# A normalisation of softmax rows moved for every fourth item from GpSimd to VectorE

## The chip, the cores and the metric

The kernel runs on one core of one Trainium2 chip. A core has TensorE (PE, matrix products), VectorE (DVE), ScalarE (ACT), GpSimd (POOL) and SyncE (SP, which here only issues DMAs). Each runs its own list of instructions in order, and they meet at semaphores. The metric is the time on the device in microseconds (us): the median of three runs is 1448.82, from 1447.1 to 1449.51.

## The reference

Four layers with a layer norm before each: graph attention over 16384 random edges and the loops, a mixture of 8 experts (top 2), a graph network, and a transformer block (attention with 8 heads, then 8 experts, top 1). The change lies in the attention of the last one. N is 1024 rows, D is 512, and a head has 64 columns:

```python
q = (x @ Wq + bq).reshape(B, S, NH, dh)      # k and v alike
scores = jnp.einsum('bqhd,bkhd->bhqk', q, k) / jnp.sqrt(jnp.float32(dh))
attn = jax.nn.softmax(scores, axis=-1)
ctx = jnp.einsum('bhqk,bkhd->bqhd', attn, v).reshape(B, S, D)
sa = ctx @ Wo + bo
x = _layernorm(x + sa, g1, beta1)            # then the experts, and a second layer norm
```

## The kernel before

Everything is computed in pairs of a high and a low half of fp32 numbers (H and L in the names), and a product is made of three products of halves. Stages follow each other; the one that matters is the second attention, from 876 to about 1172 us.

It works through 64 items. An item i is 128 queries of one head against all 1024 keys. Sixteen items (m = 0 to 15 in the code) belong to a pair of heads, hp = 0 to 3; four items with the same head and consecutive blocks make a group. Each engine has the order of its work written out by hand, in loops over hp and m that run ahead of each other by two or three items. The steps of an item:

- PE, head_scores (L1432): four matrix products into two of the banks 0 to 3 of PSUM. Done for item i + 3 while i is the current one.
- DVE, maximum (L1112): the negative row maximum, 128x1024 read from PSUM.
- ACT, head_exp (L731): the exponential into AP_[:, i % 4, :], with the row sums in denom. AP_ has four buffers.
- DVE, denominator (L1117): rden = 1 / denom, for item i + 2.
- POOL, normalise (L544): AP_ times rden, in place, 128x1024, for item i + 2.
- PE, head_transposes (L1443): eight transposes of 128x128 into banks 4 and 5. They wait for the normalisation of item i, and for the low halves of item i - 1, which empty those banks.
- ACT, head_hi (L576), and DVE, head_lo (L789): two instructions each, which copy the transposed block from PSUM to APH and the remainder to APL.
- PE, head_values (L1457, L1458, L1460): after four items, the products with V into bank 6, half of them in m % 4 == 3 and half in the next m % 4 == 0. ACT (L748) and DVE (L792, L1131) then split the result.

In between, in bank 7, PE makes what the next pair of heads needs (K in m = 1 and 3, Q in 5 and 13, V in 7 and 9, transposes of V in 10 and 11) and the output products of finished blocks; ACT and DVE split these (DVE: L792 for K and Q, L789 for V, L1135 adds the output to the residual). In the last pair of heads only outputs are left. POOL also splits the weights that the DMAs bring (L462, L466, L468), between normalisations in m = 9, 10, 14 and 15. The line helpers: L239 is every product of three passes, L789 every low half without bias.

In a round m of its loop DVE has, in this order: maximum(i + 3), denominator(i + 2), head_lo(i), and then the outputs and splits. At the end of the stage the layer norm of x (L803, L821) follows on DVE.

Of the kernel before, what the change touches and what calls it, by code (L numbers as in the profile page):

```python
# [21 lines left out]
ALU = mybir.AluOpType  # L22
# [11 lines left out]
def build(nc, a, out, ctx):  # L34
# [4 lines left out]
    HALF = N // 2  # L39
    EC = NE // P  # L40
    NEXP, _, HID = a["L0_ffn_w1"].shape
    HB = HID // P
    GB = a["L1_gnn_W1"].shape[1] // P
# [9 lines left out]
    def const(name, shape, dt):  # L53
        size = 2 if dt == F16 else 4
        for s in shape[1:]:
            size *= s
        t = nc.alloc_sbuf_tensor_at(name, shape, dt, offset=place[0])
        place[0] += (size + 31) // 32 * 32
        return t
# [34 lines left out]
    rden = const("rden", [P, 4], F32)  # L94
# [14 lines left out]
    def arena(name, shape, dt, kb):  # L109
        return nc.alloc_sbuf_tensor_at(name, shape, dt, offset=A0 + int(kb * K))  # L110
# [51 lines left out]
    AP_ = arena("AP_", [P, 4, N], F32, -16)  # L162
# [18 lines left out]
    def sem(name):  # L181
        return nc.alloc_semaphore(name)
# [14 lines left out]
    def stage_semaphores(stage, names, **rings):  # L197

        one = {n: sem(f"{stage}_{n}") for n in names.split()}
        more = {n: [sem(f"{stage}_{n}{i}") for i in range(k)] for n, k in rings.items()}  # L200
        return {**one, **more}
# [6 lines left out]
    M = stage_semaphores("moe", "lg_ps gate_dve shifted g_exp gates gt_ps gt g_ps acc h_ps hh hl y_ps", w2used=2, gelu=2, yfree=4)  # L208
    G = stage_semaphores("gnn", "hi lo eps diag chi clo ps rt_hi rt_lo h_ps mh y_ps featsum", c_in=2, relu=2, ml=2, yfree=4)
    B = stage_semaphores("att1", "bq scaled q_ps q_hi q_lo k_ps k_hi k_lo v_ps v_f vt_ps v_hi v_lo s_ps mx exp rden norm "  # L210
                         "cx_hi cx_lo y_ps yfree bias x_saved x_back", q_twice=2, t_ps=2, t_hi=2, t_lo=2, pv_ps=2)
    row0c_in = sem("row0c_in")
    F = stage_semaphores("fin", "g1 n1 g2 n2 done out")

# [200 lines left out]
    def _(gp):  # L415
        def wait(s, value):

            gp.wait_ge(s, value)
            if not isinstance(value, int):
                gp.nop(nofuse=True)  # L420
# [119 lines left out]
                split(u, u // 4, j, j, scaled=hp if j == 1 else None)  # L540

        def normalise(i):
            wait(B["rden"], i + 1)
            gp.tensor_scalar(AP_[:, i % 4, :], AP_[:, i % 4, :], rden[:, i % 4:i % 4 + 1], None,  # L544
                             ALU.mult).then_inc(B["norm"], 1)
# [3 lines left out]
        for j in range(3):  # L549
            att_split(1, j)  # L550
        normalise(0)
        normalise(1)
        for hp in range(KT):
            for m in range(2 * NT):
                i = 2 * NT * hp + m
                if i + 2 < 2 * NT * KT:
                    normalise(i + 2)
                if m == 9 and hp + 1 < KT:
                    att_split(hp + 1, 3)
                if m in (10, 14, 15) and hp + 2 < KT:  # L560
                    att_split(hp + 2, (10, 14, 15).index(m))
# [224 lines left out]
    def _(v):  # L786
# [90 lines left out]
        with v.Fori(0, 2) as i:  # L877
            for j in range(4):
# [6 lines left out]
                dst, hi_, bias = ((QL, QH, bq0), (KL, KH, bk0))[j % 2]  # L885
# [229 lines left out]
        def denominator(i):  # L1115
            v.wait_ge(B["exp"], i + 1)
            v.reciprocal(rden[:, i % 4:i % 4 + 1], denom[:, i % 4:i % 4 + 1]).then_inc(B["rden"], 1)  # L1117

        def head_lo(i):
            for half in range(2):  # L1120
                v.wait_ge(B["t_hi"][half], i + 1)
                block_ = (slice(None), slice(4 * half, 4 * half + 4), slice((i % 4) * P, (i % 4 + 1) * P))
                lo(APL[block_], PS[:, 4 + half, :].rearrange("p (k q) -> p k q", k=4), APH[block_], B["t_lo"][half])
# [18 lines left out]
        maximum(0)  # L1142
        maximum(1)
        denominator(0)
        maximum(2)
        denominator(1)
        for hp in range(KT):
            for m in range(2 * NT):
                i = 2 * NT * hp + m
                if i + 3 < 2 * NT * KT:  # L1150
                    maximum(i + 3)
                if i + 2 < 2 * NT * KT:
                    denominator(i + 2)
                head_lo(i)
                if hp and m in (0, 2, 4, 6, 8):
                    output(hp - 1, 3 + m // 2)
                if m in (12, 14, 15):
                    output(hp, (12, 14, 15).index(m))
                if hp + 1 < KT:
                    if m in (1, 3):  # L1160
                        k_lo(hp + 1, m // 2)
                    if m in (5, 13):
                        q_lo(hp + 1, m // 8)
                    if m in (10, 11):
                        v_lo(hp + 1, m - 10)
                if m % 4 == 0 and i:
                    context_lo(i // 4 - 1)
# [28 lines left out]
    def _(pe):  # L1196
# [237 lines left out]
            got.then_inc(B["s_ps"], 1)  # L1434

        def head_transposes(i):
            pe.wait_ge(B["norm"], i + 1)
            for half in range(2):
                if i:
                    pe.wait_ge(B["t_lo"][half], i)  # L1440
                for k in range(4):
                    c = 4 * half + k
                    got = pe.transpose(PS[:, 4 + half, k * P:(k + 1) * P], AP_[:, i % 4, c * P:(c + 1) * P], ident[:, :])  # L1443
                got.then_inc(B["t_ps"][half], 1)
# [91 lines left out]
        for hp in range(KT):  # L1536
            for m in range(2 * NT):
                i = 2 * NT * hp + m
                if i + 3 < 2 * NT * KT:
                    head_scores(i + 3)  # L1540
                head_transposes(i)
                if m % 4 == 0 and i:
                    head_values(i // 4 - 1, 1)
                bank7(hp, m)
                if m % 4 == 3:
                    head_values(i // 4, 0)
# [32 lines left out]
```

## Time and profile before

| | us |
|---|---|
| median of 3 runs | 1448.82 |
| profiled execution | 1446.94 |
| its span in the trace | 1444.9 |
| second attention, first maximum to last transposes | 876.5 to 1164.7 |
| PE busy in the whole span | 1068.7 (74%) |
| DVE busy | 680.9 (47%) |
| POOL busy | 671.7 (46%) |
| of it line 544, 64 times | 182.1 |
| ACT busy | 369.9 (26%) |

The shares are averages over all stages; in the second attention PE, DVE and POOL are all busy for more than two thirds of the time. The profile names a line, an engine, and "output <- inputs". A wait is put down to the instruction that ended last before it. In the timelines, a number in brackets is how long the engine sat idle before the instruction, with the one that released it; "x2" means two instructions in one row, with the time from the start of the first to the end of the last. "PEld" is PE loading weights.

### The profile page before, as it was taken

Reading aid. Unit: us, or ns where it says so; the run is one execution under the profiler, and the core shown is the slowest. Engines: PE = TensorE matmul, PEld = TensorE weight load, DVE = VectorE, ACT = ScalarE, POOL = GpSimd, SP = SyncE. Lnnn points to the kernel's source line nnn. Section 1 sums busy time; section 2 is a strip of 40 time slices with the busy share of each in tenths; the row PEclk is TensorE's granted clock in tenths of the full one; section 3 lists DMA queues with packets and bytes.
Section 4 is the critical chain, followed back from the end, with each engine's and each line's share of the span. In section 5 each row is a group of like instructions: output and inputs, shape, how many; then the busy total and the mean of one; then the engine's idle time right before and its main releaser. Section 6 shows DMA issues by size and latency. Waiting matters only on the chain.

```text
span 1444.9 us, 15065 instructions
## 1 busy us (share of the span) xinstructions
PE 1068.7 (74%) x4784; PEld 837.9 (58%) x4784; DVE 680.9 (47%) x1261; ACT 369.9 (26%) x536; POOL 671.7 (46%) x496
## 2 busy tenths in 40 slices
PE   3776991000686999994979868999998846999991
PEld 2555781000564588883867746777776624588881
DVE  7444210000565243346332276777877775244348
ACT  1111110000232112121130125666665522112120
POOL 1477777777770234310243026776857631243310
PEclk9977896555797799997999979999999986799996
DMA  9533212223550111101412022010000040111001
GB/s 283 78 30 17 1 1 0 0 0 73 169 166 0 29 44 44 50 0 44 124 37 65 0 83 56 15 44 15 23 15 15 1 137 23 29 48 54 29 0 58
DMA packets 79840, 68.85 MB, mean 48 GB/s; under 512 B 32288, under 2 KB 63264, under 8 KB 78512
## 3 DMA queue, kind: packets, MB, share of 16 engines
q1 hardware_dynamic: 60208, 68.15, 16.2%
q0 software_dynamic: 19584, 0.08, 4.1%
q8 instruction: 28, 0.46, 0.1%
q14 instruction: 20, 0.16, 0.0%
HBM read 47.17 MB, written 16.85 MB: 44 GB/s over the span
## 4 chain that ended last, share of the span: by engine, by line
PE 51%; DVE 17%; issue 13%; POOL 10%; DMA 5%; ACT 2%; SPq 1%; POOLq 1%; DVEq 0%; ACTq 0%
PE PS L239 39%; POOL edge_table L454 6%; DVE neg_max L1112 2%; DMA edge_table<-zeros 2%; PE PS L1443 2%; PE PS L1458 2%; DVE APL L789 2%; PE PS L1432 2%; PE PS L1348 2%; PE PS L1457 2%; DVE stats L803 2%; POOL index_s L448 2%; DVE XN L821 2%; DMA CT<-edge_table 1%; DMA edge_table<-count_s,index_s 1%
## 5 line engine op out<-in xcount | busy, mean ns | idle before, releaser
L466 POOL CAST WH<-RAW 128x512 fp32r<-128x512 f32 x94 | 64.4, 685 | 483.6 <-PE PS L239 382.8
L454 POOL DMA_INDIRECT edge_table<-count_s,index_s x136 | 215.9, 1588 | 71.2 <-issue 35.0
L544 POOL TENSOR_SCALAR AP__135<-AP__135,rden 128x1024 f32<-128x1024 f32 x64 | 182.1, 2849 | 85.0 <-DVE rden L1117 84.4
L239 PE MATMUL PS<-XTH,WH 128*128 128x512 f32 x480 | 169.7, 420 | 8.9 <-DVE XTL L789 6.7
L239 PE MATMUL PS<-XTL,WH 128*128 128x512 f32 x480 | 165.0, 410 | 0.0
L239 PE MATMUL PS<-XTH,WL 128*128 128x512 f32 x480 | 162.5, 405 | 0.0
L468 POOL TENSOR_TENSOR WL<-RAW,WH 128x512 fp32r<-128x512 f32 x94 | 136.8, 1456 | 11.8 <-POOL WH L466 0.2
L789 DVE TENSOR_TENSOR HL<-HF,HH 128x1024 fp32r<-128x1024 f32 x32 | 42.0, 1314 | 179.0 <-ACT HH L576 179.0
L1272 PE MATMUL PS<-ident,PR 128*128 128x128 f32 x64 | 10.4, 314 | 151.1 <-ACT PR L621 151.1
L239 PEld LDWEIGHTS PS<-XTH,WH 128*128 128x128 f32 x480 | 95.4, 202 | 33.0 <-issue 12.4
L239 PEld LDWEIGHTS PS<-XTL,WH 128*128 128x128 f32 x480 | 96.4, 201 | 20.8
L239 PEld LDWEIGHTS PS<-XTH,WL 128*128 128x128 f32 x480 | 95.6, 199 | 21.5
L657 ACT ACTIVATE HF<-PS,b 128x1024 f32<-128x1024 f32 x32 | 35.8, 1118 | 275.4 <-PE PS L239 275.4
L239 PE MATMUL PS<-WH,HH 128*128 128x512 f32 x256 | 99.6, 389 | 0.0
L239 PE MATMUL PS<-WL,HH 128*128 128x512 f32 x256 | 99.6, 389 | 0.0
L239 PE MATMUL PS<-WH,HL 128*128 128x512 f32 x256 | 99.6, 389 | 0.0
L1272 PEld LDWEIGHTS PS<-ident,PR 128*128 128x128 f32 x64 | 8.4, 162 | 153.6 <-issue 143.8
L1112 DVE TENSOR_REDUCE neg_max<-PS 128x1 f32<-128x1024 f32 x64 | 78.2, 1222 | 36.2 <-PE PS L1432 35.3
L789 DVE TENSOR_TENSOR APL<-PS,APH 128x512 fp32r<-128x512 f32 x128 | 82.9, 678 | 23.7 <-ACT APH L576 23.6
L907 DVE SCALAR_TENSOR_TENSOR CT<-CT,SR 128x1024 f32<-128x1024 f32 x8 | 9.7, 1217 | 172.2 <-POOL CT L481 172.2
L576 ACT ACTIVATE APH<-PS 128x512 fp32r<-128x512 f32 x128 | 71.8, 598 | 67.9 <-PE PS L1443 43.3
L1204 PE MATMUL PS<-ident,XN 128*128 128x128 f32 x128 | 31.2, 425 | 71.1 <-DVE XN L821 29.3
(190 smaller groups left out, 2167.9 us busy)
## 6 DMA issues: line engine op xcount, KB each, us to landing
edge_table<-zeros SPq DMA_DIRECT2D x2, 4096.0 KB, 22.9
RAW<-in_L_ffn_w SPq DMA_DIRECT2D x32, 256.0 KB
CT<-edge_table SPq DMA_DIRECT2D x16, 512.0 KB, 5.0
RAW<-in_L_ffn_W SPq DMA_DIRECT2D x32, 256.0 KB
counts<-CT SPq DMA_DIRECT2D x8, 512.0 KB, 6.0
CG<-counts SPq DMA_DIRECT2D x8, 512.0 KB, 3.3
RAW<-in_L_gnn_W SPq DMA_DIRECT2D x16, 256.0 KB
edge_table<-count_s,index_s POOLq DMA_INDIRECT x136
```

The lines of the kernel that those rows point to most:

```text
L239: got = pe.matmul(o, lhs, r, start=first and j == 0, stop=last and j == 2)
L448: gp.tensor_copy(index_s[:, par, :], index[:, ds(4 * q, 4)]).then_inc(staged, 1)
L454: gp.indirect_dma_start(out=tables[r], out_offset=bass.IndirectOffsetOnAxis(ap=index_s[:, par, c:c + 1], axis=0), in_=count_s[:, par, c:c ...
L466: gp.tensor_copy(wh, RAW[:, raw, :]).then_inc(w_hi, 1)
L468: gp.tensor_tensor(wl, RAW[:, raw, :], f(wh), ALU.subtract).then_inc(w_ready, 1)
L544: gp.tensor_scalar(AP_[:, i % 4, :], AP_[:, i % 4, :], rden[:, i % 4:i % 4 + 1], None, ALU.mult).then_inc(B["norm"], 1)
L576: act.activation(dst, src, Copy, **kw).then_inc(s, 1)
L657: act.activation(HF[:, b, :], banks(2 * b), ACT.Gelu, bias=b1[:, ds(2 * e + b)]).then_inc(M["gelu"][b], 1)
L789: v.tensor_tensor(dst, src, f(hi), ALU.subtract).then_inc(s, 1)
L803: step(v.bn_stats(stats[:, t, :], src[:, t, :]))
L1112: v.tensor_reduce(out=neg_max[:, i % 4:i % 4 + 1], in_=banks(2 * (i % 2)), axis=X_AXIS, op=ALU.max, negate=True).then_inc(B["mx"], 1)
L1204: got = pe.transpose(PS[:, t % 2, k * P:(k + 1) * P], src[:, t, k * P:(k + 1) * P], ident[:, :])
```

## The change

VectorE normalises the items with i % 4 == 3, sixteen of 64, itself, right after their reciprocal, and GpSimd leaves these out. VectorE's instruction waits for its own reciprocal and counts in a new semaphore, norm4. PE's transposes of these items wait for norm4, the others for as many of norm as GpSimd has by then made.

```diff
         def normalise(i):
+            if i % 4 == 3:
+                return
             wait(B["rden"], i + 1)
             gp.tensor_scalar(AP_[:, i % 4, :], AP_[:, i % 4, :], rden[:, i % 4:i % 4 + 1], None,
                              ALU.mult).then_inc(B["norm"], 1)
...
         def denominator(i):
             v.wait_ge(B["exp"], i + 1)
             v.reciprocal(rden[:, i % 4:i % 4 + 1], denom[:, i % 4:i % 4 + 1]).then_inc(B["rden"], 1)
+            if i % 4 == 3:
+                v.wait_ge(B["rden"], i + 1)
+                v.tensor_scalar(AP_[:, i % 4, :], AP_[:, i % 4, :], rden[:, i % 4:i % 4 + 1], None,
+                                ALU.mult).then_inc(B["norm4"], 1)
...
         def head_transposes(i):
-            pe.wait_ge(B["norm"], i + 1)
+            if i % 4 == 3:
+                pe.wait_ge(B["norm4"], i // 4 + 1)
+            else:
+                pe.wait_ge(B["norm"], i + 1 - i // 4)
             for half in range(2):
                 if i:
                     pe.wait_ge(B["t_lo"][half], i)
```

The order on VectorE in the second pair of heads, m = 0 and 1 (WH is here the context, AK the keys, AP__135 the block of probabilities). Before:

```order
513 L792 SCALAR_TENSOR_TENSOR WH<-PS,BVA,WH 64x512 [waits att1_cx_hi]
514 L1131 TENSOR_TENSOR WH<-PS,WH 64x512 [waits att1_cx_lo]
515 L1112 TENSOR_REDUCE neg_max<-PS 128x1 [waits att1_s_ps]
516 L1117 RECIPROCAL rden<-denom 128x1 [waits att1_exp]
517 L789 TENSOR_TENSOR APL<-PS,APH 128x4x128 [waits att1_t_hi0]
518 L789 TENSOR_TENSOR APL<-PS,APH 128x4x128 [waits att1_t_hi1]
519 L792 SCALAR_TENSOR_TENSOR AK<-PS,bk_68,AK 64x512 [waits att1_k_hi] x2
520 L1112 TENSOR_REDUCE neg_max<-PS 128x1 [waits att1_s_ps]
```

And now:

```order
517 L794 SCALAR_TENSOR_TENSOR WH<-PS,BVA,WH 64x512 [waits att1_cx_hi]
518 L1137 TENSOR_TENSOR WH<-PS,WH 64x512 [waits att1_cx_lo]
519 L1114 TENSOR_REDUCE neg_max<-PS 128x1 [waits att1_s_ps]
520 L1119 RECIPROCAL rden<-denom 128x1 [waits att1_exp]
521 L1122 TENSOR_SCALAR AP__135<-AP__135,rden 128x1024 [waits att1_rden]
522 L791 TENSOR_TENSOR APL<-PS,APH 128x4x128 [waits att1_t_hi0]
523 L791 TENSOR_TENSOR APL<-PS,APH 128x4x128 [waits att1_t_hi1]
524 L794 SCALAR_TENSOR_TENSOR AK<-PS,bk_68,AK 64x512 [waits att1_k_hi] x2
525 L1114 TENSOR_REDUCE neg_max<-PS 128x1 [waits att1_s_ps]
```

The multiplication of item 19 (L1122) stands between its reciprocal and the two low halves of item 17; the low halves, the key halves and the maximum behind it are one place later.

On GpSimd, the first pair of heads, with the splits of weights (WL and WH from RAW) between the normalisations. Before:

```order
150 L544 TENSOR_SCALAR AP__135<-AP__135,rden 128x1024 [waits att1_rden] x12
151 L466 CAST WL<-RAW 128x512 [waits raw_in3]
152 L468 TENSOR_TENSOR WL<-RAW,WL 128x512 [waits w_hi]
153 L544 TENSOR_SCALAR AP__135<-AP__135,rden 128x1024 [waits att1_rden]
154 L466 CAST WH<-RAW 128x512 [waits raw_in0,att1_k_ps]
155 L468 TENSOR_TENSOR WL<-RAW,WH 128x512 [waits w_hi]
156 L544 TENSOR_SCALAR AP__135<-AP__135,rden 128x1024 [waits att1_rden] x4
```

And now:

```order
150 L546 TENSOR_SCALAR AP__135<-AP__135,rden 128x1024 [waits att1_rden] x9
151 L466 CAST WL<-RAW 128x512 [waits raw_in3]
152 L468 TENSOR_TENSOR WL<-RAW,WL 128x512 [waits w_hi]
153 L546 TENSOR_SCALAR AP__135<-AP__135,rden 128x1024 [waits att1_rden]
154 L466 CAST WH<-RAW 128x512 [waits raw_in0,att1_k_ps]
155 L468 TENSOR_TENSOR WL<-RAW,WH 128x512 [waits w_hi]
156 L546 TENSOR_SCALAR AP__135<-AP__135,rden 128x1024 [waits att1_rden] x3
```

Three of twelve, and one of the four behind the second split, have gone; the splits keep their places among the rest.

## Rows read from the trace of the kernel before

**Rows 1.** Waits, 876 to 1166 us: waiter, releaser: us in total, times, longest us.

```profile
POOL AP__135 L544 <- DVE rden L1117: 84.4, 38, 4.7
...
DVE neg_max L1112 <- PE PS L1432: 35.3, 20, 3.9
...
PE PS L1443 <- DVE APL L789: 11.1, 15, 2.2
...
PEld PS L1443 <- POOL AP__135 L544: 1.4, 2, 0.7
```

**Rows 2.** Windows: us, busy us of PE, PEld, DVE, ACT, POOL; clock; DMA.

```profile
950.00:1020.00 70.00, 66.09 (x344) 51.92 (x343) 53.87 (x85) 41.54 (x73) 51.68 (x25) 1.00 0.10 27
```

**Rows 3.** Chain of waits, around item 19: start us, us, what.

```profile
961.08 0.02 issue
...
963.09 0.17 DVE rden L1117
963.25 1.18 DVE APL L789 x2
...
964.47 0.74 DVE AK L792
...
967.46 0.60 DVE APL L789
...
968.19 1.16 PE PS L1443 x8
```

**Rows 4.** Timeline of DVE around items 3, 7, 11, 23, columns as in group 3.

```profile
891.49 0.75 DVE L792 SCALAR_TENSOR_TENSOR AK<-PS,bk,AK 64x512 fp32r<-64x512 f32 x1 [1.85 <-ACT AK L715]
...
910.21 1.53 DVE L792 SCALAR_TENSOR_TENSOR AQL<-PS,bq1s,AQH 64x512 fp32r<-64x512 f32 x2 [0.34 <-ACT AQH L708]
...
929.09 1.23 DVE L1112 TENSOR_REDUCE neg_max<-PS 128x1 f32<-128x1024 f32 x1 [0.26 <-PE PS L1432]
...
982.36 1.27 DVE L789 TENSOR_TENSOR APL<-PS,APH 128x512 fp32r<-128x512 f32 x2
983.76 1.53 DVE L792 SCALAR_TENSOR_TENSOR AQL<-PS,bq1s,AQH 64x512 fp32r<-64x512 f32 x2
```

**Rows 5.** Groups of DVE by shape, whole kernel: busy us, mean ns.

```profile
L821 DVE TENSOR_SCALAR XN<-X,mv,rstd 128x512 f32<-128x512 f32 x32 | 15.0, 540 | 0.1
...
L1117 DVE RECIPROCAL rden<-denom 128x1 f32<-128x1 f32 x64 | 10.0, 156 | 1.8 <-ACT AP__135 L731 1.2
...
L1179 DVE TENSOR_TENSOR XN<-XN,rows 128x512 f32<-128x512 f32 x16 | 9.8, 678 | 0.0
```

**Rows 6.** Timeline of POOL and DVE around items 3 and 19.

```profile
883.86 8.50 POOL L544 TENSOR_SCALAR AP__135<-AP__135,rden 128x1024 f32<-128x1024 f32 x3 [0.41 <-DVE rden L1117]
...
888.30 0.15 DVE L1117 RECIPROCAL rden<-denom 128x1 f32<-128x1 f32 x1
...
960.11 2.85 POOL L544 TENSOR_SCALAR AP__135<-AP__135,rden 128x1024 f32<-128x1024 f32 x1
```

**Rows 7.** Line 821 at 1182 us: min/median/max ns; then POOL in the same stretch.

```profile
L821 DVE TENSOR_SCALAR XN<-XN,mv,rstd x8: 542/830/1487, 1182.7 to 1188.6; 128x512 f32<-128x512 f32 x8
...
1184.21 1.31 POOL L468 TENSOR_TENSOR WL<-RAW,WH 128x512 fp32r<-128x512 f32 x1
```

**Rows 8.** Timeline around the last item.

```profile
1160.58 2.85 POOL L544 TENSOR_SCALAR AP__135<-AP__135,rden 128x1024 f32<-128x1024 f32 x1 [1.94 <-DVE rden L1117]
1161.36 1.16 PE L1443 MATMUL PS<-ident,AP__135 128*128 128x128 f32 x8 [2.20 <-DVE APL L789]
...
1162.71 1.29 DVE L789 TENSOR_TENSOR APL<-PS,APH 128x512 fp32r<-128x512 f32 x2 [0.91 <-ACT APH L576]
...
1163.55 0.83 PE L1443 MATMUL PS<-ident,AP__135 128*128 128x128 f32 x5 [0.34 <-POOL AP__135 L544]
```

**Rows 9.** One window, columns as in group 2, and PE at its start.

```profile
1128.00:1132.00 4.00, 3.15 (x12) 2.89 (x13) 3.67 (x8) 2.92 (x5) 3.79 (x2) 0.60 0.00 0
...
1128.85 1.94 PE L1443 MATMUL PS<-ident,AP__135 128*128 128x128 f32 x8 [1.85 <-DVE APL L789]
```

More of the change, by code:

```diff
@@ L210, in build @@
     B = stage_semaphores("att1", "bq scaled q_ps q_hi q_lo k_ps k_hi k_lo v_ps v_f vt_ps v_hi v_lo s_ps mx exp rden norm "
-                         "cx_hi cx_lo y_ps yfree bias x_saved x_back", q_twice=2, t_ps=2, t_hi=2, t_lo=2, pv_ps=2)
+                         "cx_hi cx_lo y_ps yfree bias x_saved x_back norm4", q_twice=2, t_ps=2, t_hi=2, t_lo=2, pv_ps=2)
     row0c_in = sem("row0c_in")
```

## The prediction

> **What bounds the kernel now.** I read the table of waits for the stage of the second attention first, then busy time by window, then the chain of waits, and last the timelines around the items that change. "Item i" is one head and one block of 128 queries (64 in all); a "group" is four items.
>
> The waits [rows 1] look like a reason for the change only at first. GpSimd (POOL) waits 84.4 us for the reciprocal of VectorE (DVE), so it has time to spare, and PE waits for a normalised block 1.4 us in all. PE waits for the low halves of line 789, which DVE makes, 11.1 us in the same stage. The window in the middle of the stage [rows 2] shows PE busy for 66.09 of 70 us and DVE for 53.87 us, about 77%, at full clock (1.00, 2.4 GHz). POOL has 51.68 of 70.
>
> An average of 77% would leave DVE 16 us free per 70. The reader should look at where they are. The chain [rows 3] shows a pattern that returns in each group of four: a long burst on DVE without a gap (context, maximum, reciprocal, low halves, K or Q low halves, maximum, reciprocal, low half), and at its end PE starts the transposes of the next item (968.19) the moment the first low half is there. From there on PE works alone (a projection, the values, the scores) and DVE idles, mostly before line 1112, 35.3 us in 20 waits [rows 1]. The two engines take turns on the chain, and the reciprocal of every item with i % 4 == 3 stands in the middle of DVE's turn.
>
> **The change part by part.** Own time of the profiled execution: 1446.94 us, of which the span is 1444.9; the median of the runs is 1448.82, 1.88 more. I add the sum to the median; the offset does not matter.
>
> *Removed from POOL:* 16 of 64 normalisations of 2.85 us [rows 6], 45.6 us. POOL waits 84.4 us already, so this is worth what PE waited for it, at most 1.4 us in two waits plus 0.34 us at the end [rows 1, 8].
>
> *The last item* looks like a gain: the chain passes through its normalisation, 1160.58 to 1163.43, before the transposes at 1163.55 [rows 8]. But the transposes also need the first low half of item 62, which DVE starts at 1162.71 and has about 0.67 us later, at 1163.38. That follows from PE's transposes at 1161.36, which waited 2.20 us for the low half of item 61, and in the new order the normalisation of item 63 stands ahead of just that low half. So the item gains some 0.03 us and is delayed as any other: I count it among the full ones.
>
> *Added on DVE:* 16 times, between the reciprocal of item i and the low halves of item i - 2, one tensor_scalar of 128x1024. I call what it puts into DVE's row X. No row shows this shape there. The nearest is the same operation on 128x512: 540 ns, and 15.0 us for 32, which is 0.47 us from one to the next, so 0.07 us overlap with the neighbour [rows 5]. A tensor_tensor of the same shape takes 678 ns [rows 5]. Below: the double width costs nothing more, D = 0.54 us. Above: it doubles everything, D = 1.08. I take the middle, D = 0.81, since the 128x512 form is already quicker than the tensor_tensor, and part of it is fixed. It also waits for the reciprocal of its own engine: that takes 0.17 us and a dependent instruction follows after 0.02 to 0.03 us of issue [rows 3], where the low half used to start beside it, 0.07 to 0.08 us after its start. That adds about 0.10 to 0.12. X = 0.81 - 0.07 + 0.10 = 0.84 us, with bounds 0.57 and 1.11.
>
> The Trainium skill ("VectorE: DVE Perf Modes", section "Mode 2x_2P") says that a one-source operation on fp32 from SBUF to SBUF handles two elements a cycle. By that 512 more elements would take 0.27 us more, D = 0.81, the same value; the 0.47 us spacing for 512 columns agrees, as it is below 512 cycles at that page's 0.96 GHz.
>
> *What X hides under.* Only a gap of DVE between the new instruction and the hand-over to PE can take it. The gaps [rows 4]: item 3, 1.85 us (it waits for ACT's K half after a projection); item 7, 0.34; item 11, 0.26; items 15, 23, 31, 39 and 47 have the shape of 982.36: the low halves end at 983.63 and the Q halves start at 983.76, 0.13. The other eight (19, 27, 35, 43, 51, 55, 59, 63) have next to nothing: at item 19 the low halves end at 964.43 and the K halves start at 964.47 [rows 3]. Behind the hand-over PE is continuously busy until DVE's next turn, so nothing is caught up there.
>
> *Item 3 and the other engine's port.* Later in the kernel the 128x512 tensor_scalar takes 542 to 1487 ns, median 830, while POOL runs its splits, such as one of 1.31 us [rows 7]; alone it takes 540 [rows 5]. So the two slow each other: the instruction waits about until POOL's is over. In the attention this bites if POOL is in the middle of a normalisation when DVE's starts. At item 3 it is: three run in a row from 883.86 to 892.36 (items 1, 2 and 3), so that of item 2 runs from about 886.7 to 889.5, and the reciprocal of item 3 is at 888.30 [rows 6]. The new instruction would run from about 889.5 to 890.4, the low halves end at 891.7, 0.2 us after 891.49. I count 0.2. At item 19 POOL's previous one ends at 962.96, just before the reciprocal at 963.09 [rows 3, 6], and elsewhere it ends sooner, since items come some 6 us apart there. POOL held up by DVE costs nothing.
>
> The Trainium skill ("SBUF — State Buffer", section "Who interferes with whom") has it as a lock: of a VectorE operation in a two-port mode and a GpSimd operation, the second waits until the first is over. The trace agrees, with the 1487 ns. By that rule the sum stays as it is as long as POOL is done, and it is what the third rival below has more of.
>
> *Sum of the row:* 0.2 for item 3; 15 X = 12.6 for the others, less 0.34, 0.26 and 5 x 0.13 = 0.65, in all 1.25. That is 11.55 us, with bounds 7.5 (X = 0.57) and 15.6 (X = 1.11).
>
> *PE's clock.* PE's waits at these places become longer by about X. In the last head pair PE already waits 1.85 us for a low half at 1128.85, and just behind it the granted clock is 0.60 on average over 4 us, partly the lower level of 1.2 GHz; the eight transposes take 1.94 us where 1.16 is usual [rows 8, 9]. The wait of 2.20 at 1161.36 has no such effect [rows 8]. So it is not sure to come; one drop costs 0.78 us in the transposes and, by the same factor on what follows in that window, about 0.5 more, 1.3 us. I add one, with bounds of none and four: 0 to 5.2.
>
> Total: 11.55 + 1.3 = 12.85, so **1448.8 + 12.9 = 1461.7 us**, 0.9% slower. Own range 1456.3 (7.5 and no drop) to 1469.6 (15.6 and four drops, 20.8).
>
> **The rivals.**
>
> *Hidden after all (not slower).* DVE idles 35.3 us before the maximum [rows 1] and the 16 new instructions need 13.4. If the hand-over at the end of DVE's burst were not what PE waits for, but the work of PE itself, all of it would fit into these gaps, and what remains is the 1.4 + 0.3 us that PE waited for POOL: 1447.1. It decides from the point where PE's transposes behind the burst start later for another reason than the low half, by 0.84 us or more. For it: PE is the busiest engine [rows 2]. Against it: the chain enters PE at 968.19 straight from the low half at 967.46 [rows 3].
>
> *Partly hidden.* The chain has near-equals: where the scores or ACT's copies come at nearly the same time, a slip of X counts for half. Then 1448.8 + 5.8 = 1454.6. For it: the gaps that I read are of one execution, and two paths that come 0.1 to 0.3 us apart change places easily. Against it: eight of 16 places have no gap.
>
> *Collision on the port.* DVE's delay moves the group, and POOL's splits stand between its normalisations; if at item 19 and its like (19, 35), where 0.13 us separates the end of POOL's from the reciprocal, and a few others the new instruction meets a running one, it waits up to 2.85 us [rows 6]. Six places with half of that, 1.4 us each, give 8.5 on top: 1470. For it: the 1487 ns [rows 7]. Against it: POOL has one instruction less to do in each group and waits 38 times for DVE [rows 1].
>
> **How the numbers follow.** Chances: the forecast 0.60, the collision or a heavier clock loss (above 1469) 0.14, partly hidden (1451.7 to 1456) 0.15, wholly hidden 0.11, of which 0.07 lie within 0.2% (2.9 us, about what a measurement here can tell from no change) and 0.04 below, faster. Slower: 0.60 + 0.14 + 0.15 = 0.89. The range for 8 in 10 takes in the forecast's, and a third or so of the partly hidden case: 1454.5 to 1469.6.
>
> **What would show it right or wrong.** Right: the stage from the first maximum to the last low half is some 12 us longer and no other is; the new instruction takes 0.8 us, except at item 3, where it takes about 1.9; PE's wait for line 789 rises from 11.1 us by about 10; POOL's wait grows although it has less to do; DVE's share in the middle of the stage rises to about 80%; POOL no longer ends a wait of PE. Wrong: a tensor_scalar of 1.1 us or more (then the size is off), durations of 2 us and more at many items (the port), or PE's waits unchanged (hidden).

## The result and the profile after

The changed kernel takes 1459.23 us (median of 14 runs, 1450.78 to 1462.92) against 1447.83 of the kernel before in as many runs: 11.4 us more. The ratio is 1.0079, with a 95% interval of 1.0059 to 1.0098, so it is slower. One execution of all that are counted here and below ran in a slow state (2618 us, among the twelve of e4_left_out) and is left out of the ratios. The prediction was 1461.7, or 12.9 us more than the median that it started from. The profiled execution has a span of 1457.2 us, 12.3 more than before.

The page after, first section (busy time, share, instructions):

```profile
PE 1075.1 (74%) x4784; PEld 840.1 (58%) x4784; DVE 693.2 (48%) x1277; ACT 370.9 (25%) x536; POOL 627.2 (43%) x480
```

DVE has 12.3 us more than before and 16 instructions more, POOL 44.5 us less. The waits of the second attention, in the columns of [rows 1]:

```profile
POOL AP__135 L546 <- DVE rden L1119: 135.3, 32, 8.1
...
DVE neg_max L1114 <- PE PS L1438: 36.4, 20, 3.9
...
PE PS L1452 <- DVE APL L791: 15.9, 19, 3.0
```

The line numbers are the changed kernel's. POOL waits 135.3 us for the reciprocals where it waited 84.4, though it has 16 fewer to work on. PE's transposes wait 15.9 us for the low halves, 11.1 before; the products with V wait 10.2 us for them, 10.6 before. Part of PE's longer wait probably stands under "issue", time for which the profile names no cause: 27.2 us in front of weight loads of the transposes, 16.8 before. The wait for POOL is gone from the list. DVE idles before the maximum as long as before, 36.4 and 35.3 us: the new work has not gone into that gap.

The window that answers to [rows 2]:

```profile
950.00:1020.00 70.00, 64.72 (x330) 49.48 (x331) 54.06 (x85) 41.27 (x73) 43.10 (x21) 1.00 0.12 31
```

The same 70 us hold less work of PE, 64.72 for 66.09, at the same full clock; DVE's share is 77% as before. The new instruction and what POOL has left of its own (durations in ns, min/median/max, and the first and last start in us):

```profile
L1122 DVE TENSOR_SCALAR AP__135<-AP__135,rden x16: 752/753/1598, 889.5 to 1172.3; 128x1024 f32<-128x1024 f32 x16
```

```profile
L546 POOL TENSOR_SCALAR AP__135<-AP__135,rden x48: 2845/2848/2867, 881.7 to 1167.5; 128x1024 f32<-128x1024 f32 x48
```

VectorE's instruction takes 0.75 us, fifteen times of sixteen; the 1.60 us are those of item 3. Around item 19 the timeline of DVE and PE reads, where before it was [rows 3]:

```profile
965.44 0.16 DVE L1119 RECIPROCAL rden<-denom 128x1 f32<-128x1 f32 x1
...
965.64 0.75 DVE L1122 TENSOR_SCALAR AP__135<-AP__135,rden 128x1024 f32<-128x1024 f32 x1
...
966.31 1.28 DVE L791 TENSOR_TENSOR APL<-PS,APH 128x512 fp32r<-128x512 f32 x2
967.14 1.16 PE L1452 MATMUL PS<-ident,AP__135 128*128 128x128 f32 x8 [0.33 <-DVE APL L791]
...
967.62 1.53 DVE L794 SCALAR_TENSOR_TENSOR AK<-PS,bk,AK 64x512 fp32r<-64x512 f32 x2
...
969.18 1.23 DVE L1114 TENSOR_REDUCE neg_max<-PS 128x1 f32<-128x1024 f32 x1
...
970.44 0.16 DVE L1119 RECIPROCAL rden<-denom 128x1 f32<-128x1 f32 x1
...
971.34 1.16 PE L1452 MATMUL PS<-ident,AP__135 128*128 128x128 f32 x8 [0.25 <-DVE APL L791]
```

And the reciprocals of items 0 and 20 in the kernel before, for comparison:

```profile
880.33 0.16 DVE L1117 RECIPROCAL rden<-denom 128x1 f32<-128x1 f32 x1 [1.23 <-ACT AP__135 L731]
...
967.29 0.17 DVE L1117 RECIPROCAL rden<-denom 128x1 f32<-128x1 f32 x1
```

From the reciprocal of item 19 to that of item 20 it was 4.20 us (963.09 to 967.29), now it is 5.00. The difference of 0.80 is what the new instruction costs here: it begins at 965.64, 0.04 us after the end of the reciprocal, and the low halves begin at 966.31 instead of beside the reciprocal. K halves and maximum follow at once, and so do PE's transposes at the end.

**The slip of each item.** Since the order of work is fixed, this comparison can be made for all items: the start of item i's reciprocal, counted from that of item 0, in one kernel less in the kernel before. I call it the slip. It leaves out the stages ahead, in which executions differ by some us. "Layer norm" is the start of the layer norm's first statistics (line 803 before, 805 now). In the change:

| item | 4 | 8 | 12 | 16 | 20 | 24 | 28 | 32 | 36 | 40 | 44 | 48 | 52 | 53 | 54 | 56 | 60 | 63 | layer norm |
|---|---|---|---|---|---|---|---|---|---|---|---|---|---|---|---|---|---|---|---|
| slip, us | 0.01 | 0.36 | 0.81 | 1.29 | 2.10 | 2.67 | 3.30 | 3.78 | 4.61 | 5.20 | 5.83 | 6.31 | 7.12 | 8.74 | 9.10 | 9.90 | 10.70 | 10.69 | 12.38 |

It never falls back by more than 0.12 us, and it grows once in each group, right behind the item with i % 4 == 3: by 0 at item 3, by 0.36 to 0.65 where something of it is hidden, by 0.80 at items 19, 35, 51, 55 and 59. At items 53 and 54 it grows by 2 us without a new instruction. There, two windows (columns of [rows 2]) and PE's transposes in the first of them show

```profile
1118.00:1122.00 4.00, 1.48 (x7) 1.51 (x8) 3.93 (x6) 1.50 (x3) 0.00 (x0) 0.70 0.00 2
1122.00:1126.00 4.00, 4.00 (x14) 3.22 (x13) 2.67 (x6) 1.99 (x4) 2.85 (x1) 0.50 0.00 0
...
1120.52 1.94 PE L1452 MATMUL PS<-ident,AP__135 128*128 128x128 f32 x8 [2.62 <-DVE APL L791]
```

that PE had waited 2.62 us, and that the granted clock fell to 0.50, the lower level of 1.2 GHz. The eight transposes take 1.94 us instead of 1.16. The same happened once in the profile of the kernel before, at item 54 [rows 9]. In the changed kernel's profile it happened twice more, at items 54 and 62:

```profile
1138.00:1142.00 4.00, 2.20 (x10) 2.06 (x11) 3.96 (x8) 2.23 (x4) 0.46 (x1) 0.76 0.00 0
...
1174.00:1178.00 4.00, 4.00 (x20) 3.46 (x20) 2.31 (x4) 1.45 (x3) 0.00 (x0) 0.57 0.00 0
```

The first of these answers to the drop before and does not show in the slip; the second is part of the last step, 1.69 us from item 63 to the layer norm. From the first reciprocal to the layer norm the stage is 12.38 us longer. What lies ahead of it takes 1.05 us more (881.38 for 880.33) and what lies behind it 1.09 us less in these two executions, so the two cancel and the stage has all of the 12.3 us.

### The profile page after: what moved, and what is told of

Read it like the earlier page. It is cut to its first block, busy times and chain, and to the rows that moved or that the text cites. A ratio compares the mean times of both kernels' runs of the same rounds, so it can differ in the third digit from the quotient of the medians.

```text
span 1457.2 us, 15065 instructions
## 1 busy us (share of the span) xinstructions
PE 1075.1 (74%) x4784; PEld 840.1 (58%) x4784; DVE 693.2 (48%) x1277; ACT 370.9 (25%) x536; POOL 627.2 (43%) x480
## 4 chain that ended last, share of the span: by engine, by line
PE 48%; DVE 20%; issue 12%; POOL 10%; DMA 5%; ACT 2%; SPq 1%; POOLq 1%; DVEq 0%; ACTq 0%
PE PS L239 37%; POOL edge_table L454 6%; DVE APL L791 3%; DVE neg_max L1114 3%; DMA edge_table<-zeros 2%; PE PS L1467 2%; PE PS L1452 2%; PE PS L1354 2%; PE PS L1466 2%; DVE stats L805 2%; POOL index_s L448 2%; DVE XN L823 2%; DMA edge_table<-count_s,index_s 2%; PE PS L1438 2%; DMA CT<-edge_table 1%
## 5 line engine op out<-in xcount | busy, mean ns | idle before, releaser
L546 POOL TENSOR_SCALAR AP__135<-AP__135,rden 128x1024 f32<-128x1024 f32 x48 | 136.7, 2850 | 136.1 <-DVE rden L1119 135.3
L1278 PE MATMUL PS<-ident,PR 128*128 128x128 f32 x64 | 10.4, 316 | 151.2 <-ACT PR L623 151.1
L1114 DVE TENSOR_REDUCE neg_max<-PS 128x1 f32<-128x1024 f32 x64 | 78.2, 1222 | 37.1 <-PE PS L1438 36.4
L1452 PE MATMUL PS<-ident,AP__135 128*128 128x128 f32 x512 | 74.2, 288 | 16.5 <-DVE APL L791 15.9
```

Of the source, the lines that this page charges most:

```text
L1114: v.tensor_reduce(out=neg_max[:, i % 4:i % 4 + 1], in_=banks(2 * (i % 2)), axis=X_AXIS, op=ALU.max, negate=True).then_inc(B["mx"], 1)
```

## Experiments

Each ran beside the kernel before, in five rounds. The interval of such a ratio is 0.2 to 0.4% to either side, 3 to 5 us; the slips are read from one profiled execution of each kernel, and repeat within 0.1 us between executions as long as the clock is the same (the change once more: 0.29, 1.22, 2.61, 3.74, 6.21 at items 8, 16, 24, 32, 48).

**e1_idle_place.** VectorE takes the items i % 4 == 1, in the gap. Item 1 alone is done directly behind its reciprocal, before the loop starts. The first lines of the cut are in GpSimd's normalise, the others in VectorE's loop; norm_dve is the wait and the tensor_scalar of the change as a function of their own, and PE's waits count to match.

```diff
-            if i % 4 == 3:
+            if i % 4 == 1:
                 return
...
                 head_lo(i)
+                if m % 4 == 3 and i + 2 < 2 * NT * KT:
+                    norm_dve(i + 2)
```

> VectorE normalises sixteen items again, but those with i % 4 == 1, and not after their reciprocal: behind the low halves of the round m % 4 == 3, where VectorE then idles 2 to 3.9 us because TensorE works alone. Theory (the cost is the place in VectorE's burst): the stage is as long as before, -1 to +1.5 us against the kernel before; each instruction 0.75 us, no collision. Rival (work on VectorE costs wherever it stands, or the move off GpSimd costs by its semaphores or the shared port): again about +11 us. Rival (relief of GpSimd is worth something): faster by up to 1.7 us.

Measured: ratio 0.9997 (0.9979 to 1.0015). The slip is between -0.09 and +0.29 up to item 56, and the layer norm begins 1.0 us earlier than before, because the drop of the clock at item 54 is missing here. Sixteen instructions of the same kind on the same engine, relieving the same other engine, cost nothing. So it was neither the engine nor the semaphore, but the place in the row. That none would collide was wrong. Five of them met an instruction of GpSimd: three a normalisation, and took 1.28, 1.50 and 1.50 us, two a split of weights, and took 0.86. One of the first kind:

```profile
L1123 DVE TENSOR_SCALAR AP__135<-AP__135,rden x16: 744/746/1495, 879.4 to 1146.3; 128x1024 f32<-128x1024 f32 x16
```

```profile
1002.43 2.85 POOL L546 TENSOR_SCALAR AP__135<-AP__135,rden 128x1024 f32<-128x1024 f32 x1
...
1004.33 1.50 DVE L1123 TENSOR_SCALAR AP__135<-AP__135,rden 128x1024 f32<-128x1024 f32 x1
```

GpSimd's instruction ends at 1005.28, VectorE's at 1005.83, after 1.50 us instead of 0.75; in the gap none of these costs anything.

**e2_item1_early.** The same items, directly behind their reciprocal (in the change's code, 3 becomes 1).

> The same items i % 4 == 1 on VectorE, but directly after their reciprocal, where GpSimd is still in the normalisation of the item before in about half of the places. Theory with the port (VectorE's tensor_scalar waits until GpSimd's instruction is over): durations from 0.75 to about 2.8 us, single ones above 2 us at items 13, 29 and 45; in the rounds m = 3 and 7 it hides behind a projection on TensorE, in 11 and 15 and in the last pair of heads it delays the values: about +14 us. Rival without the port: all durations 0.75 us, and the same places give about +7 us. If the place does not matter at all: +11 us as in the change.

Measured: ratio 1.0121 (1.0098 to 1.0144), 16.7 us by the medians (1460.38 and 1443.73); the slip at the layer norm is 16.3 us. So the place matters, and the sum was near, but by luck, since the mechanism that I gave is not there: no instruction took over 2 us.

```profile
L1122 DVE TENSOR_SCALAR AP__135<-AP__135,rden x16: 753/791/1272, 878.1 to 1160.0; 128x1024 f32<-128x1024 f32 x16
```

```profile
948.00:952.00 4.00, 3.27 (x8) 2.19 (x9) 1.78 (x3) 0.07 (x1) 3.77 (x5) 0.57 0.06 17
...
948.73 0.77 PE L1467 MATMUL PS<-APH,AV 128*128 128x512 f32 x1 [2.02 <-DVE APL L791]
```

Behind item 17 the values on PE wait 2.02 us, and then run at a mean clock of 0.57. The slip rises by 2.54 us there, of which the instruction accounts for about 1; at items 29, 45, 49 and 53 it rises by 2.3 to 2.5. The trace has seven such stretches of lower clock, and by these steps they are more than half of the cost of this kernel.

**e3_dummy_1024.** GpSimd as before; VectorE has an additional instruction at the places of the change.

```diff
             v.reciprocal(rden[:, i % 4:i % 4 + 1], denom[:, i % 4:i % 4 + 1]).then_inc(B["rden"], 1)
+            if i % 4 == 3:
+                v.wait_ge(B["rden"], i + 1)
+                v.tensor_scalar(MF[:, 1, 0:1024], MF[:, 0, 0:1024], rden[:, i % 4:i % 4 + 1], None,
+                                ALU.mult).then_inc(B["norm4"], 1)
```

> GpSimd normalises all 64 items as in the kernel before; VectorE has at the places of the change a tensor_scalar of 128x1024 on a buffer that nobody else uses, with the same wait for its reciprocal. Theory: what is added on VectorE is all of the cost, +11 to +13 us. Rival (the changed handover between engines, or the lighter GpSimd, has a part): clearly less or more than the change's 11.4 us.

Measured: ratio 1.0089 (1.0064 to 1.0114), 12.5 us by the medians. The slips are those of the change to 0.1 us up to item 52: 0.30, 1.23, 2.67, 3.80 and 6.26 at items 8, 16, 24, 32, 48. The addition on VectorE alone is the whole cost. Here GpSimd starts its normalisation of the same item 0.06 us after VectorE's instruction, at fifteen of the sixteen places. VectorE is not delayed (0.75 us), and GpSimd takes 3.41 us instead of 2.85 without any effect on the slips.

**e4_left_out.** The counterpart: GpSimd leaves the items out, and nobody normalises them; PE's transposes of these items wait for the reciprocal instead.

> The items with i % 4 == 3 are normalised by nobody (that part of the computation is left out), otherwise as the change. Theory: relief of GpSimd is worth nothing but the start and the last item, -0.6 to 0 us against before. Rival (the waits of TensorE for GpSimd, 1.4 and 0.34 us, are all given back): -1.7 us or more.

Measured: ratio 0.9995 (0.9974 to 1.0016). The slips are 0.07 us or less at every item, and the layer norm begins 295.37 us after the first reciprocal, in the kernel before 295.41. The relief of GpSimd is worth nothing, not even the 0.34 us at the end.

**e5_after_low.** The items of the change in the same round, but behind the low halves.

```diff
                 head_lo(i)
+                if m % 4 == 1:
+                    norm_dve(i + 2)
```

> The items of the change (i % 4 == 3), in the same round m % 4 == 1, but behind the two low halves instead of ahead of them. Theory (the whole burst of VectorE is on the chain, not only the low half that releases TensorE's transposes): the Q and K halves and the maximum behind are still 0.8 us later, so +8 to +10 us against before; the transposes in the last pair of heads no longer wait longer than before, so the clock's part (2 us) goes. Rival (only the low half is waited for): 0 to +2 us.

Measured: ratio 1.0033 (1.0010 to 1.0057), 4.2 us by the medians, and a slip of 6.57 us at item 63. The interval, 1.4 to 8.2 us, leaves room for both expectations, but the slip fits neither: it costs, so the rest of the burst is on the chain too, but less than I expected. The timeline behind item 23 tells why:

```profile
986.57 0.15 DVE L1119 RECIPROCAL rden<-denom 128x1 f32<-128x1 f32 x1
986.63 1.27 DVE L791 TENSOR_TENSOR APL<-PS,APH 128x512 fp32r<-128x512 f32 x2
987.82 0.74 DVE L1123 TENSOR_SCALAR AP__135<-AP__135,rden 128x1024 f32<-128x1024 f32 x1
988.48 1.52 DVE L794 SCALAR_TENSOR_TENSOR AQL<-PS,bq1s,AQH 64x512 fp32r<-64x512 f32 x2
```

The reciprocal is over by 986.72, long before 987.82, so nothing waits for it. The low halves start 0.06 us after it again, and the instruction adds 0.66 us to the row (987.82 to 988.48). The step at items 20, 36, 52, 56 and 60 is 0.66 us here and 0.80 in the change: the wait for the own reciprocal is 0.14 us of X. That the clock's part would go was not met: the granted clock falls three times in the last pair of heads here too, behind waits of 1.8 us as before, but each time costs only 0.2 to 0.4 us.

**e6_dummy_512.** As e3_dummy_1024, with 0:512 for 0:1024.

> As the extra tensor_scalar at the places of the change with GpSimd as before, but 128x512. Theory: it takes 0.46 to 0.54 us, X is about 0.5 us; 15 X less the gaps of 1.25 us, and about one clock drop: +6 to +9 us. Rival (a fixed price for each instruction and its wait, whatever its size): the same as with 128x1024, about +11 us.

```profile
L1120 DVE TENSOR_SCALAR MF<-MF,rden x16: 486/486/1367, 883.8 to 1159.8; 128x512 f32<-128x512 f32 x16
```

Measured: ratio 1.0037 (1.0016 to 1.0058), 5.2 us by the medians, below the lower end of what I expected, though the interval reaches up to 8.4 and excludes only the rival's 11; the slips are 0.02, 0.42, 1.28, 1.85, 3.25 at items 8, 16, 24, 32, 48 and 3.88 at item 63, and the step at the places without a gap is 0.53. The cost goes with the size: 0.486 us for 512 columns and 0.753 for 1024, 0.27 for 512 more. Where there was a gap, about half of this small X is gone in it (at item 7 all but about 0.1).

**e7_not_last_pair** and **e8_last_pair_only.** The change for i < 48 and for i >= 48.

```diff
-            if i % 4 == 3:
+            if i % 4 == 3 and i < 48:      # the other: i >= 48
```

> The change in the first three pairs of heads only (12 items on VectorE). Theory: the slips read from the trace up to item 48 add to +6.3 us, without any change of the clock: +5.5 to +7 us. Rival (cost in proportion to the number of instructions): 12 of 16 of 11.4 us, +8.5 us.

> The change in the last pair of heads only (4 items on VectorE). Theory: no gaps there, 4 x 0.8 us, and 1 to 3 us by one to three drops of the granted clock behind longer waits of TensorE: +4.2 to +6.2 us. Rival (in proportion): +2.9 us. Rival (no clock): +3.2 us.

Measured: ratios 1.0052 (1.0032 to 1.0073) and 1.0032 (1.0009 to 1.0056), 7.3 and 5.3 us by the medians. The layer norm slips by 7.64 and 4.74, together 12.38, which is the change's to the last digit (by luck, since the clock has a part in it). The first has a slip of 6.32 at item 48, the change 6.31, and that is the range that I expected; the times alone (4.6 to 10.6 us for e7, 1.3 to 8.1 for e8) exclude none of the rivals. By the traces, the twelve instructions cost 0.53 us each up to item 48, and the four 1.2 each, clock included. The clock's part is not tied to the new instructions: in e7 nothing is added in the last pair and PE's waits there are those of the kernel before, 1.8 to 2.2 us, and yet the clock falls three times and adds 1.3 us to the slip behind item 48.

**e9_collide.** GpSimd does a normalisation of nothing at the items of the change, from the exponential on.

```diff
             if i % 4 == 3:
+                wait(B["exp"], i + 1)
+                gp.tensor_scalar(MF[:, 1, :], MF[:, 0, :], MF[:, 0, 0:1], None,
+                                 ALU.mult).then_inc(B["norm5"], 1)
                 return
```

> The change, and for its sixteen items GpSimd makes a 128x1024 tensor_scalar of its own on an unused buffer, which starts as soon as the exponential is there, about 1 us or more before VectorE's normalisation. Theory of the shared port: VectorE's instruction ends about 0.55 us after the end of GpSimd's (as it did at the change's item 3), so it takes 1.5 to 3 us instead of 0.75, and the kernel is slower than the change by 10 to 30 us. Rival (the 1.6 us at item 3 had another cause): 0.75 us at all items but the first, and the change's +11.4 us.

Measured: ratio 1.0130 (1.0101 to 1.0159), 19.1 us by the medians, 7.9 more than the change on the same chip (1453.9); slip 9.68 at item 48, 3.4 more. VectorE's instruction:

```profile
L1125 DVE TENSOR_SCALAR AP__135<-AP__135,rden x16: 752/1086/1636, 886.5 to 1173.0; 128x1024 f32<-128x1024 f32 x16
```

Of four of them, each with GpSimd's instruction ahead of it (start, us, engine):

```profile
905.03 3.36 POOL L545 TENSOR_SCALAR MF<-MF 128x1024 f32<-128x1024 f32 x1 [0.72 <-ACT AP__135 L736]
...
906.74 0.75 DVE L1125 TENSOR_SCALAR AP__135<-AP__135,rden 128x1024 f32<-128x1024 f32 x1
...
962.57 2.85 POOL L545 TENSOR_SCALAR MF<-MF 128x1024 f32<-128x1024 f32 x1
...
962.92 1.31 DVE L1125 TENSOR_SCALAR AP__135<-AP__135,rden 128x1024 f32<-128x1024 f32 x1
...
981.21 2.85 POOL L545 TENSOR_SCALAR MF<-MF 128x1024 f32<-128x1024 f32 x1 [0.72 <-ACT AP__135 L736]
...
983.52 1.09 DVE L1125 TENSOR_SCALAR AP__135<-AP__135,rden 128x1024 f32<-128x1024 f32 x1
...
1171.95 2.84 POOL L545 TENSOR_SCALAR MF<-MF 128x1024 f32<-128x1024 f32 x1 [0.83 <-ACT AP__135 L736]
...
1173.00 0.75 DVE L1125 TENSOR_SCALAR AP__135<-AP__135,rden 128x1024 f32<-128x1024 f32 x1
```

Both theories miss. The two engines do hold each other up, but beyond item 3, where it was so in the change too, VectorE's delay is 0.3 to 0.56 us at twelve places and nothing at three, not 1 to 2: in the third case VectorE starts 2.31 us after GpSimd and ends at 984.61, 0.55 us after GpSimd's end at 984.06. In the second it starts 0.35 us after it, waits 0.56 us, and is done at 964.23, while GpSimd goes on until 965.42. In the fourth it starts 1.05 us after it, and neither is delayed. In the first it starts 1.71 us after it and is not delayed, but GpSimd's takes 3.36 us instead of 2.85.

**e10_fill** and **e11_before_fill.** TensorE multiplies while it waits, in the last pair of heads; the second is the same in the kernel before, with range(5).

```diff
+            if i >= 48 and i % 4 == 2:
+                pe.wait_ge(B["cx_lo"], 2 * (i // 4))
+                for n in range(8):
+                    pe.matmul(PS[:, 6, :], AQH[:, 0, 0:P], AK[:, 1, 0, 0:HALF], start=True, stop=True)
             for half in range(2):
```

> The change, and in the last pair of heads TensorE makes eight matrix products whose result nobody uses (1.9 us) in front of the transposes of each item i % 4 == 2, where it waits 2.6 us for VectorE. Theory (the slip of items 52 to 54 in the change, 2 us beyond X, is the lower clock behind the longer wait): no stretch below 0.9 granted clock in the last pair; the last reciprocal is 8.0 to 9.0 us later against the first than in the kernel before, not 10.7. Rival (the slip there has another cause): still about 10.7 us, or more by the added products.

> The kernel before, with five such products in the last pair of heads, where it waits 1.8 us. Theory: the clock stays up at item 54, where it fell in the profile of before; 0 to 1.3 us less, below what the times can tell. Rival (the added products are themselves on the chain): +1 to +4 us.

The last pair of heads in the first of them, item 50's transposes and two windows of the place that fell before:

```profile
1112.50 1.25 PE L1456 MATMUL PS<-ident,AP__135 128*128 128x128 f32 x8 [0.67 <-DVE APL L791]
...
1108.00:1112.00 4.00, 3.68 (x18) 2.48 (x16) 3.84 (x7) 2.80 (x6) 0.00 (x0) 1.00 0.00 0
1112.00:1116.00 4.00, 3.50 (x23) 2.97 (x23) 4.00 (x8) 2.49 (x7) 1.66 (x1) 1.00 0.01 2
```

No stretch of the last pair is below full clock, and the slip at item 54 is 6.96 us, where the change has 9.10: the 2 us are gone. At item 63 it is 7.59, a little below what I expected (8.0 to 9.0), because the kernel before had a drop of its own in its profile: against e11_before_fill, whose slip is between -0.14 and -0.07 from item 6 to 56 and about -1.07 from 57 to 63, it is 8.66, and 9.34 at the layer norm (304.06 and 294.72 us after the first reciprocal). That is the cost of the change without the clock, to about 0.1 us: at item 62 the added products run 0.3 to 0.4 us past the low half in both kernels, and so are themselves on the chain there. The times can't tell this apart: 1.0064 (1.0042 to 1.0085) beside the 1.0091 of e12, and 1.0007 (0.9987 to 1.0026) for e11, so there is no version here that is measurably faster than the kernel before.

**e12_change_again.** The change unchanged.

> The change once more, unchanged, as the measure for the others on this chip: +0.6 to +1.0%; slips of 0.80 us at items 20, 36 and 52 as before; stretches of lower clock in the last pair of heads where TensorE waits 2.6 us or more, not necessarily at the same items.

Measured: ratio 1.0091 (1.0055 to 1.0127), 11.2 us by the medians. The steps at items 20, 36 and 52 are 0.80 again. The slip at item 54 is 7.01, at 63 7.89 and at the layer norm 9.32: this execution had no drop behind item 51, two slighter ones later. So the clock's part differs by 3 us between two profiled executions of one kernel. The six executions of this run go from 1450.80 us at a mean granted clock of 0.863 to 1462.69 at 0.856.

## Why the prediction was right

*That DVE's burst, not its average, is the bound*: shown. e3 has the full cost with GpSimd as before, e1 none with VectorE as loaded as in the change.

*The relief of GpSimd*, priced at 1.4 + 0.34 us at most: worth nothing (e4). PE's waits for POOL gave way to another.

*The last item* as a normal one: right. The slip grows by 0.68 us between item 63 and the layer norm in e10 against e11, where the chain of waits would suggest that it shrinks.

*X*: 0.84 was predicted, 0.80 measured. D is 0.753 us (predicted 0.81), and the wait for the reciprocal 0.14 (predicted 0.10). The Trainium skill ("VectorE: DVE Perf Modes", "Mode 2x_2P") has two fp32 elements a cycle for this operation; the 0.27 us for 512 more columns agree with it.

*The gaps*: the term of the sum that was mis-sized. I took 0.34 and 0.26 for items 7 and 11, five times 0.13, and none for eight items, in all 1.25 us. From the steps of e10 against e11 (0.38, 0.33, 0.59, 0.79, 0.57, 0.54, 0.59, 0.80, 0.59, 0.50, 0.60, 0.80, 0.80, 0.80 and 0.68 at the fifteen items from 7 to 63) they are 0.42, 0.47, about 0.2 at the five with the Q halves, and 0.26 and 0.30 at items 27 and 43, which I had counted as full: 2.5 us in all, twice what I took. The idle time between two instructions, in brackets or from their ends, is too small by about 0.1 us, since an instruction that has not to wait starts up to 0.09 us before the end of the one ahead of it. At items 11, 27 and 43, 0.11 us of this is hidden one item later, where the low half began 0.17 us after the start of its reciprocal and now begins 0.07 after it. The steps add to 9.36 us, where I had 11.55 with item 3's 0.2; item 3 costs nothing.

*The clock*: one drop of 1.3 us was added, and it is 3.7 us in the profiled execution (13.07 - 9.36, against e11), and near 0.7 in e12 (10.01 - 9.36, same way). The medians differ by 11.4 and 11.2, so if all that the row leaves is the clock's, it is about 2 us in the mean. The two errors cancel in part, and so far the closeness is luck: the row 2.2 too much, the clock about 0.7 too little.

*The port*: at item 3 the instruction took 1.60 us, where I had about 1.9, and GpSimd's was the reason, as predicted:

```profile
887.73 2.85 POOL L546 TENSOR_SCALAR AP__135<-AP__135,rden 128x1024 f32<-128x1024 f32 x1
...
889.53 1.60 DVE L1122 TENSOR_SCALAR AP__135<-AP__135,rden 128x1024 f32<-128x1024 f32 x1
```

That GpSimd is done elsewhere was right too. The rival "collision" would have cost less than its 8.5 us, as e9 shows: with a delay at nine places up to item 48 beside item 3 it comes to 3.4 us. The Trainium skill ("SBUF — State Buffer", "Who interferes with whom") says that the one that is second waits for the whole instruction of the other; here VectorE waited 0.88 us at most (item 3 of e9), in a GpSimd instruction of 2.85, and three of the e9 cases (items 7, 11 and 63) overlapped without any delay of VectorE. The measurement decides: one of the two waits only for a part of the other's instruction. That what they share is held in parts of GpSimd's instruction is my reading of these cases.

*Partly hidden* had something to it, through the larger gaps, and *hidden* had nothing: DVE's idle time before the maximum is unchanged.

*The signs*: three were off. PE's listed wait for the low halves rose by 4.8 us and not by 10 (10.4 more stand under "issue"), DVE's share in the middle stayed at 77% where I had 80%, since the stage grows with the work, and item 3 took 1.60 us.

What stays open: why the clock falls at one place in one execution and at another in the next. In these profiles every stretch of lower clock in the stage, but for the one at its start, begins during a wait of PE of 1.7 us or more, or up to 1.5 us behind it. The length of the wait does not decide: 2.61 us in the profile after had no such effect, e7 has three drops behind waits no longer than before, and e1 has those same waits and no drop. So one profile of e10 without a drop could be chance; beside it stand the mean clocks of whole executions, 0.863 to 0.868 in the nine of e10 and 0.856 to 0.864 in the six of e12. That keeping PE busy prevents the drops is likely, then, but rests on this. For the kernel before it gained nothing that shows (e11: 0.861 to 0.868, before: 0.860 to 0.866).

## What to carry to other kernels

An engine at 77% can be on the chain with every microsecond of the wrong 77%: before moving work to it, mark on its timeline where it is idle within one period, and put the work there (e1, free) rather than where its input becomes ready (the change, 11 us). An engine that nobody waits for is worth nothing relieved, and a row of the chain that names it may only be first among equals. Where TensorE has waits of 2 us, allow for stretches of its lower clock behind them, which a moved instruction can add or shift: about 2 us of 11 in the change, more than half of the cost in e2.

## What the runs showed of the hardware

- VectorE's tensor_scalar, fp32 in SBUF, with a scalar from memory, one operation: 0.486 us for 128x512 and 0.753 for 128x1024; the 128x512 form with two scalars from memory takes 0.540.
- Waiting for one's own previous result costs 0.14 us between reciprocal and tensor_scalar, which is avoided with two independent instructions between them (e5).
- GpSimd's 128x1024 tensor_scalar of 2.85 us and VectorE's of 0.75 overlap freely if VectorE's starts 1.05 us after GpSimd's. If it starts 0.35 or 2.3 us after it, it is delayed by 0.3 to 0.56 us, at 1.76 us (item 3 of e9) by 0.88. At 1.7 us (items 7 and 11 of e9), or if it starts 0.06 us ahead of GpSimd's (e3), VectorE's is not delayed and GpSimd's takes 3.33 to 3.41 us.
- TensorE's granted clock fell from 2.4 to 1.2 GHz during or just behind waits of 1.7 to 3.0 us inside an otherwise busy stage, in some executions and not in others. Such a stretch cost from 0.2 us (e5) to about 2 (item 50 of the change).
